# Layer 0's output before its last product: rows split into float16 parts and turned by DMA instead of turned on TensorE in single precision

## What is computed

```
y = elu(rgcn_conv(norm_x, edges, types_2))     # (625, 286)
y = y @ wo_weight                              # (286, 1024)
x = layernorm(x + (x + y))                     # input of layer 1, "x1" below
u = x1 @ root + bias + sum_r mean_r(x1) @ weight[r]      # layer 1, 8 relations
h = tanh(u) * z + x1 * (1 - z),  z = concat(u, x1) @ w_gate + b_gate
out = layernorm(x1 + (x1 + h))
```

## Time and profile before

| | us |
|---|---|
| median of 3 runs (lowest to highest) | 856.54 (856.15 to 856.7) |
| the profiled execution's own time | 857.1 |
| its span, first to last instruction | 855.3 |
| PE busy | 818.4 (96%) |
| DVE busy | 677.6 (79%) |
| ACT busy | 437.4 (51%) |
| DMA queue q1 | 66.71 MB, 24.2% of 16 engines' span |

### The profile page before, as it was taken

The page is one execution under the profiler, slowest core; times in us unless marked ns, Lnnn a source line. Parts: engine busy times, 40 slices in busy tenths (PEclk is TensorE's granted clock), DMA queues, the critical chain, the costliest instruction groups (busy, mean ns, idle before and its releaser), DMA issues.

```text
span 855.3 us, 15873 instructions
## 1 busy us (share of the span) xinstructions
PE 818.4 (96%) x6276; PEld 581.4 (68%) x6276; DVE 677.6 (79%) x972; ACT 437.4 (51%) x608; POOL 15.6 (2%) x38
## 2 busy tenths in 40 slices
PE   3699999999999999999999999999999999999996
PEld 1366664448858677686686776867868768678544
DVE  6899689899787777777867777778677687788996
ACT  3576755745663553545535545456255453554711
POOL 2000000000000000000000000000000000000000
PEclk9699999999999999999999999999999999999998
DMA  9100166802202202202022021120220211306811
GB/s 310 61 1 2 47 231 175 215 1 99 99 2 99 99 2 99 71 28 98 0 98 98 0 98 53 45 98 0 98 98 0 98 39 61 123 1 143 203 49 72
DMA packets 51628, 68.72 MB, mean 80 GB/s; under 512 B 22166, under 2 KB 25874, under 8 KB 51587
## 3 DMA queue, kind: packets, MB, share of 16 engines
q1 hardware_dynamic: 50199, 66.71, 24.2%
q10 hardware_dynamic: 1388, 1.44, 0.5%
HBM read 57.71 MB, written 5.18 MB: 74 GB/s over the span
## 4 chain that ended last, share of the span: by engine, by line
PE 82%; DVE 9%; ACT 4%; issue 2%; DMA 2%; ACTq 0%; SPq 0%; DVEq 0%; POOL 0%; POOLq 0%
PE psP L1112 46%; PE psA L1178 20%; PE psP L952 12%; PE psA L941 3%; DMA stage<-in_L_gnn_W_rel 1%; PE psP L1044 1%; DVE p_mem L1389 1%; ACT wsplit L655 1%; DVE wsplit L1456 1%; DVE wsplit L1352 1%; DVE p_mem L1390 1%; PE psP L912 1%; DVE xT L1317 1%; ACT cu_mem L660 0%; ACT cu_mem L687 0%
## 5 line engine op out<-in xcount | busy, mean ns | idle before, releaser
L1112 PE MATMUL psP<-wsplit,xT 128*128 128x256 f16 x2592 | 294.7, 273 | 0.8 <-DVE p_mem L1647 0.8
L1112 PEld LDWEIGHTS psP<-wsplit,xT 128*128 128x128 f16 x2592 | 253.5, 98 | 34.0 <-DVE p_mem L1647 1.0
L1178 PE MATMUL psA<-p_mem,cu_mem 128*128 128x512 f16 x800 | 175.4, 379 | 1.9 <-DVE cu_mem L1631 1.9
L1112 PE MATMUL psP<-wsplit,x 128*128 128x256 f16 x1296 | 150.3, 273 | 0.0
L1178 PEld LDWEIGHTS psA<-p_mem,cu_mem 128*128 (+1 forms) x800 | 78.2, 98 | 93.2 <-DVE cu_mem L1631 2.4
L1112 PEld LDWEIGHTS psP<-wsplit,x 128*128 128x128 f16 x1296 | 126.8, 98 | 14.7
L1352 DVE SCALAR_TENSOR_TENSOR wsplit<-stage,sc,wsplit 128x1024 f16<-128x1024 f32 x90 | 114.7, 1279 | 26.1 <-ACT wsplit L655 26.1
L655 ACT ACTIVATE wsplit<-stage,sc 128x1024 f16<-128x1024 f32 x90 | 100.6, 1137 | 14.6 <-DVE sc L1247 8.7
L1631 DVE SCALAR_TENSOR_TENSOR cu_mem<-psA,coef,cu_mem 128x512 f32<-128x512 f32 x80 | 60.0, 750 | 32.1 <-PE psA L1178 30.3
L655 ACT ACTIVATE wsplit<-x,sc 128x1024 f16<-128x1024 f32 x54 | 61.8, 1144 | 44.4 <-PE psP L1112 31.6
L1352 DVE SCALAR_TENSOR_TENSOR wsplit<-x,sc,wsplit 128x1024 f16<-128x1024 f32 x54 | 69.2, 1282 | 11.1 <-ACT wsplit L655 10.9
(11 more groups left out here) (203 smaller groups left out, 785.7 us busy)
## 6 DMA issues: line engine op xcount, KB each, us to landing
stage<-in_L_gnn_weight SPq DMA_DIRECT2D x16, 2048.0 KB, 7.8
stage<-in_L_gnn_w_gate SPq DMA_DIRECT2D x4, 2048.0 KB, 7.8
x_home<-x SPq DMA_DIRECT2D x5, 512.0 KB, 3.2
x<-x_home SPq DMA_DIRECT2D x5, 512.0 KB, 5.7
x<-in_x SPq DMA_DIRECT2D x4, 512.0 KB, 9.8
xT<-in_L_gnn_root SPq DMA_DIRECT2D x1, 2048.0 KB, 9.0
stage<-in_L_gnn_root SPq DMA_DIRECT2D x1, 2048.0 KB, 7.7
out<-x SPq DMA_DIRECT2D x4, 512.0 KB
```

The lines of the kernel that those rows point to most:

```text
L1112: last = nc.tensor.matmul(psP[:, bank, (col + tt) * FB:(col + tt + 1) * FB], lhs[tt](a, c), split_block(n, b)[:, c, :], start=(first and t ...
L1178: last = nc.tensor.matmul(psA[:, (NT * h + t) % 2, :], cnt8[:, r, s, t * P:(t + 1) * P], p_part[h][a][:, s, :], start=(s == 0 and a == 0), ...
```

## The change

The three single-precision transposes a tile leave PE. ACT writes the high float16 part of a tile of y in row form from `acc0` (SBUF), DVE writes the rest beside it (`y_rows`, in the upper part of `p_mem`), and SP turns both parts of a tile with one DMA (128x768 float16) into `yT`. `wo_product(t)` waits for that DMA. `y_low` of tiles 0 and 1 moves ahead of `agg0_add(3)` and `wo_low`; `y_low` of tiles 2, 3 and 4 stands behind `elu_end(2, NT)` and ahead of `unit_scale(U_ROOT, 0)`. On ACT `y_high` of tiles 0 and 1 moves ahead of the exponentials of tiles 2 and 3, and that of tile 4 ahead of `raw_high(U_ROOT, 0)`. On SP tiles 0 and 1 are turned before the load of the root weights' second half, tiles 2 to 4 after `load(U_REL, 0, ...)`. On PE `degrees8(5, 7)` moves from behind `wo_product(3)` to behind `wo_product(1)`.

```diff
+        y_rows = p_mem[:, 2 * NT * HALF - FC * NPAD:2 * NT * HALF].bitcast(F16).rearrange("p (t a f) -> p t a f", t=NT, a=2)
...
-        y_turned = sem("y_turned")
+        yT_ready = [sem(f"yT_ready{t}") for t in range(NT)]
...
             sp.dma_start(vec[:, :], b1_d.partition_broadcast(P)).then_inc(bias_loaded, 16)
+
+            def turn_y(t):
+
+                sp.wait_ge(y_lo, t + 1)
+                sp.dma_start_transpose(yT[:, :, :, t * P:(t + 1) * P].rearrange("p a c n -> p (a c) n"),
+                                       y_rows[:, NT - 1 - t, :, :].rearrange("p a f -> p (a f)")).then_inc(yT_ready[t], 16)
+
+            turn_y(0)
+            turn_y(1)
             sp.wait_ge(wo_lo, 1)
             load(U_ROOT + 1, 1, by_chunk(root_d[:, HALF:D]))
             sp.wait_ge(agg0_full, NT * R0)
             w1_v = w1_d.rearrange("r (c p) f -> p (r c) f", p=P)
             sp.wait_ge(wsum_ready, 5)
             load(U_REL, 0, w1_v[:, 0:DC, 0:HALF])
+            for t in range(2, NT):
+                turn_y(t)
...
             def y_high(t):
-                act.wait_ge(y_turned, t + 1)
-                nc.scalar.activation(yT[:, 0, :, t * P:(t + 1) * P],
-                                     psA[:, t % 2, 0:FPAD].rearrange("p (c n) -> p c n", c=FC), ACT.Copy).then_inc(y_hi, 1)
-
-            for t in range(NT - 1):
-                elu_exponential(t)
+                act.wait_ge(y_ready, t + 1)
+                nc.scalar.activation(y_rows[:, NT - 1 - t, 0, :], acc0[:, t, :], ACT.Copy).then_inc(y_hi, 1)
+
+            elu_exponential(0)
+            elu_exponential(1)
             y_high(0)
             y_high(1)
+            elu_exponential(2)
+            elu_exponential(3)
             weight_sum(U_ROOT, 0, slot_load(U_ROOT), parts=(0, 1))
             elu_exponential(NT - 1)
             weight_sum(U_ROOT, 0, slot_load(U_ROOT), parts=(2, 3))
-            y_high(2)
-            y_high(3)
+            for t in range(2, NT):
+                y_high(t)
             raw_high(U_ROOT, 0)
-            y_high(4)
...
-                act.wait_ge(y_turned, NT)
+                act.wait_ge(y_lo, NT)
...
-            def turn_y(t):
-                pe.wait_ge(y_ready, t + 1)
-                if t >= 2:
-                    pe.wait_ge(y_lo, t - 1)
-                for c in range(FC):
-                    last = nc.tensor.transpose(psA[:, t % 2, c * P:(c + 1) * P], acc0[:, t, c * P:(c + 1) * P], ident[:, :])
-                last.then_inc(y_turned, 1)
-
...
-                pe.wait_ge(y_hi, t + 1)
-                pe.wait_ge(y_lo, t + 1)
+                pe.wait_ge(yT_ready[t], 16)
...
             aggregate0(NT - 2)
-            turn_y(0)
-            turn_y(1)
             aggregate0(NT - 1)
             degrees8(2, 5)
             wo_product(0)
-            turn_y(2)
-            turn_y(3)
             wo_product(1)
-            turn_y(4)
+            degrees8(5, 7)
             wo_product(2)
             wo_product(3)
-            degrees8(5, 7)
             wo_product(4)
...
             def y_low(t):
                 dve.wait_ge(y_hi, t + 1)
-                tt(yT[:, 1, :, t * P:(t + 1) * P], psA[:, t % 2, 0:FPAD].rearrange("p (c n) -> p c n", c=FC),
-                   yT[:, 0, :, t * P:(t + 1) * P], ALU.subtract).then_inc(y_lo, 1)
+                tt(y_rows[:, NT - 1 - t, 1, :], acc0[:, t, :], y_rows[:, NT - 1 - t, 0, :], ALU.subtract).then_inc(y_lo, 1)
 
             agg0_add(0)
             agg0_add(1)
             elu_end(0, 2)
             agg0_add(2)
+            y_low(0)
+            y_low(1)
             agg0_add(3)
             wo_low()
-            y_low(0)
-            y_low(1)
             agg0_add(4)
             elu_end(2, NT)
+            for t in range(2, NT):
+                y_low(t)
             unit_scale(U_ROOT, 0)
-            y_low(2)
-            y_low(3)
...
             x1_factors(0)
-            y_low(4)
             wo_add(1, 0)
```

## The result

The changed kernel takes 860.8 us (median of 5 runs, 860.41 to 861.54), the kernel before 856.54 (855.75 to 858.25): a ratio of 1.005, with a 95% interval of 1.0036 to 1.0065. It is slower by 4.3 us; 4.4 were forecast (860.9), and the range was 857.5 to 863.4.

What follows compares the result with a forecast made beforehand. The first root product's start (144.17) was taken to set the end. Tile 2's landing 134.2 + PE work 12.4 + clock 2.0 = 148.6, 4.4 us late: 856.54 + 4.4 = 860.9 us, range 857.5 to 863.4.

Steps and rivals of the forecast that it cites:

- The hold on the queue: SP's queue: y's tiles 2 to 4 wait behind two 2 MB loads; PE idles 6.5 us, 127.7 to 134.2.
- The landing: y's third transpose (tile 2) lands at 134.2, from 132.6 + 1.2 + 0.4; bounds 132.4 to 135.4.
- The transpose's own time: On the DMA engines: 128x1024 took about 1.6 us (28 slices), so 768 columns take 1.2, at about 215 GB/s.
- The clock: PE's granted clock falls to 1.2 GHz after the 6.5 us idle; cost 2.0 us, between 1.6 and 3.2.
- The rival that it stays up: Transposes held but PE's clock not falling: first root product at 146.6, time 859.0; chance 0.15.
- The sum as a whole: First root product at 134.2 + 12.4 + 2.0 = 148.6, 4.4 us after 144.17; time 860.9.
- The shift carries over in full: After the first root product: later stages shift by the same; wrong if PE's waits after 200 us shrink.
- The cost-free parts: y's tiles 0 and 1 land by 118.3, early y_low fills DVE's 0.66 us wait, tiles 3 and 4 hide.
- x1's gate: DVE's path to x1's first tile: root product could start at 144.5, by this gate alone 0.3 us late.
- The first rival: SP's queue: transposes pass or share with the loads, tile 2 lands by 132.1; time 856.8; chance 0.12.
- The third: Queue does not hold and ACT's table load is hidden, DVE 0.55 us ahead at wo_add(1, 0): 856.0; chance 0.03.
- The fourth: Tile 2 lands at 135.4 and the clock costs more than 3.2 us: above 863.4; chance 0.04.

Runs made afterwards that it cites:

- the filled kernel: Changed kernel with plain copies for all 25 DMA transposes and 28 unread matmuls on PE ahead of wo_product(2): 858.8 us, ratio 1.0032.
- the experiment with one move: Changed kernel with plain copies for all 25 DMA transposes, y's tiles 2 to 4 issued ahead of the relation's load: 857.11 us, ratio 1.001.
- the last experiment: The experiment with one move, plus unit_scale(U_ROOT, 0), raw_low, last degrees and x1's store reordered for x1's first tile: 855.84 us, ratio 0.9997.

## Why the prediction was right

Its steps and what they measured, in the clock of the kernel before (1.21 us added to the times of after):

| step | forecast | measured |
|---|---|---|
| `wo_low` ends | 118.5 | 118.6 |
| y's third transpose issued | 124.0 | 124.2 |
| second load landed | 132.9 | 133.5 |
| y's third transpose landed | 134.2 | 134.3 |
| PE idle ahead of `wo_product(2)` | 6.5 | 6.59 |
| cost of the clock | 2.0 | 1.9 in the stretch, 2.0 by the filled kernel |
| x1's first transpose issued | 139.8 | 140.0 |
| first root product starts | 148.6 | 149.0 |

- **The hold on the queue** is the main term, and it was right for the reason given: a DMA waits for what was issued ahead of it on SP's queue. The landing behind loads was the row to read. Two experiments bear it out, 10.14 us for a plain copy in the same place and 4.5 us with one load fewer. Whether it is the queue's order alone or the DMA engines' work, which comes in the same order, they do not part.
- **The landing** is made up of two misses. The sum has the load land at 132.9, 10.7 us after an issue at 122.2, and the transpose 1.3 us behind it. The load landed at 133.5, 11.1 us after issue, and the transpose 0.8 us behind it. The two misses cancelled: that the landing fits to 0.1 us is partly luck.
- **The transpose's own time**: the row of slices has 26 with traffic, not 28, so 128x1024 took some 1.5 us and not 1.6, a tenth too much in the sum. Nor does transposing explain the slow pace. In the experiment with one move the plain copies of y's tiles, in the same 256-byte pieces, moved at 219 to 231 GB/s (125 to 127 us), against the 215 read from the earlier trace rows and the 390 of a load.
- **The clock**: one stretch near the start gave the size well. The rival that it stays up had 0.15; it falls by the windows above, and its price, 859.0, is nearly what the filled kernel takes, 858.8.
- **The sum as a whole** came out 0.4 us short of these two executions (4.4 forecast, 4.8 measured): 0.1 at the landing, 0.14 from there to PE's restart, which the sum leaves out, and 0.1 in PE's work behind it. That the medians of the first measurement fit to 0.1 us is luck in part as well, as those of the later ones show (4.7).
- **The shift carries over in full**: PE's waits from 200 us on stayed at 1.9 and 0.8 us.
- **The cost-free parts**: y's first two tiles landed 2.8 us after issue and PE went from the degrees to `wo_product(0)` with no wait. The two early `y_low` filled DVE's wait; `wo_low` came 0.35 us later, for 0.25 forecast. The last two tiles caused no wait.
- **x1's gate**: the forecast was 0.3 us late; it was 0.5 (139.99 against 139.51), with the wait for ACT's table load and square root in its place. It was hidden, as PE came later:

```profile
130.58 0.16 DVE L1549 RECIPROCAL rstd<-std 128x1 f32<-128x1 f32 x1 [0.45 <-ACT std L759]
```

- **The first rival** (transposes pass the loads) falls by the 10.1 us. The third (PE's relief comes through, 856.0) had its two conditions tried in the last experiment, and even with both, and more moved, the time was that of before (855.84 against 856.06). The fourth (the worst of both ends) falls by the landing at 134.3 and the clock's 1.9 us.

What the prediction did not go into is that taking the hold away does not by itself make the kernel faster than before. DVE's path to the bank and to x1's first tile stays the gate, and PE, early at it, waits there, in one execution with the clock falling behind that wait.

## What to carry to other kernels

When work moves from an engine to a DMA, look at what is queued ahead of it, not at the length of the transfer: here some 1.1 us of data (estimated from the earlier trace rows) took 10.1 us because 4 MB of loads had been issued first, which ACT first read at 147.2 us. A wait of PE has a second price behind it, the clock: here 2 us on top of 6.6, and filling the wait with useless matmuls bought them back. And relief for a busy engine is worth little in a stretch that waits for another; PE was rid of 2.2 us of transposes here, while DVE's path to x1's first tile set the start of the next stage.

## What the runs showed of the hardware that had not been expected

- Issuing slows too behind loads. SP took 1.33 us to issue y's first transpose and 3.61 for the third, 9.24 for the three behind the loads. Three plain copies took 7.26 us there, and 2.02 with one load fewer ahead. SP had nothing urgent then, but a DMA to be issued behind them would have been late. The last load ahead of them landed 14.8 us after the issue of the first load, against 14.4 before.
- The clock fell not only in the idle time of 6.6 us but in single executions after waits of 0.90 and 2.10 us, and near 38 us in the execution of before after one of 1.48. None of these waits decides alone: one of 0.98 us behind the same 50 one-column matmuls left the clock at 1.00 in another execution, and so did one of 1.49 near 37 us in that of the changed kernel. Why it falls in one execution and not in the next was not tested.
- Executions of one kernel differed by up to 2.5 us (856.09 to 858.56), as much as the effects looked for. The profiled one was at the upper end there, so its stretch must not be read as the typical one. That of the kernel before (857.1) was above the median too, as its clock fell once more at 38 us.
